# Local attention: weights split and stacked before the turn back, one spread matmul a shift, output read from PSUM, all query products on VectorE

## What is computed

```python
q = pointwise(Wq, bq, x); k = pointwise(Wk, bk, cond); v = pointwise(Wv, bv, cond)
k = pad(k, left 8, right 7); v = pad(v, left 8, right 7)
idx = arange(T)[:, None] + arange(16)[None, :]
k_win = k[:, :, idx].reshape(B, H, hd, T, W)
v_win = v[:, :, idx].reshape(B, H, hd, T, W)
dots = einsum('bhdt,bhdtw->bhtw', qh, k_win) * scale
attn = softmax(dots, axis=-1)
out = einsum('bhtw,bhdtw->bhdt', attn, v_win)
return pointwise(Wo, bo, out)
```

## Time and profile before

| | |
|---|---|
| median of 3 runs | 1247.41 us (1245.87 to 1249.03) |
| span of the profiled execution | 1249.7 us |
| VectorE busy | 958.3 us (77%) |
| TensorE matmuls | 1111.4 us (89%) |
| ScalarE | 290.6 us (23%) |
| GpSimd | 453.1 us (36%) |
| mean granted TensorE clock | 0.958 |

### The profile page before, as it was taken

One profiled execution on the slowest core, in us unless ns is written; L12 is line 12 of the kernel. 1 busy time (PEld: TensorE's weight loads), 2 busy tenths in 40 slices (PEclk: granted clock), 3 DMA queues, 4 the chain that ended last, 5 costly groups with the idle time before them and its releaser, 6 DMA issues. The chain is left out here.

```text
span 1249.7 us, 14398 instructions
## 1 busy us (share of the span) xinstructions
PE 1111.4 (89%) x5022; PEld 803.6 (64%) x5022; DVE 958.3 (77%) x1510; ACT 290.6 (23%) x442; POOL 453.1 (36%) x303
## 2 busy tenths in 40 slices
PE   5888888867778899998999989999999869999998
PEld 1433333334556777876778767877777646777687
DVE  5999999959977878877878778887887756666423
ACT  2222222113211222222222222232222221111122
POOL 5455555535515433432434233342442011112121
PEclk8899999888889999999999999999999969999999
DMA  8000000000301111101111011100100001212001
GB/s 266 1 1 3 1 2 1 9 9 11 105 28 34 52 34 35 52 7 47 34 34 37 15 52 35 34 32 20 61 7 1 1 17 53 65 54 56 14 1 68
DMA packets 45071, 43.26 MB, mean 35 GB/s; under 512 B 6574, under 2 KB 33974, under 8 KB 45004
## 3 DMA queue, kind: packets, MB, share of 16 engines
q1 hardware_dynamic: 44284, 41.70, 10.8%
q10 hardware_dynamic: 720, 0.63, 0.1%
HBM read 40.22 MB, written 2.10 MB: 34 GB/s over the span
## 5 line engine op out<-in xcount | busy, mean ns | idle before, releaser
L1171 POOL TENSOR_TENSOR shared<-shared 128x512 f32<-128x512 f32 x80 | 103.0, 1287 | 181.5 <-DVE shared L1298 181.5
L1176 POOL TENSOR_TENSOR s<-s,c_mx 128x256 f32<-128x256 f32 x64 | 39.3, 615 | 217.7 <-DVE c_mx L1315 217.7
L699 PE MATMUL ps<-woh,oh 128*128 128x512 f32 x256 | 104.8, 409 | 7.8 <-DVE ol L1345 7.6
L369 POOL TENSOR_TENSOR r<-r 128x1024 f32<-128x1024 f32 x32 | 77.3, 2417 | 88.8 <-DVE r L508 88.7
L700 PE MATMUL ps<-xl,wqh 128*128 128x512 f32 x256 | 102.1, 399 | 5.7 <-issue 5.7
L699 PE MATMUL ps<-xh,wqh 128*128 128x512 f32 x256 | 106.1, 414 | 0.4 <-DVE shared L1298 0.4
L701 PE MATMUL ps<-xh,wql 128*128 128x512 f32 x256 | 101.8, 398 | 0.0
L700 PE MATMUL ps<-wol,oh 128*128 128x512 f32 x256 | 101.2, 395 | 0.0
L701 PE MATMUL ps<-woh,ol 128*128 128x512 f32 x256 | 101.2, 395 | 0.0
L1329 DVE TENSOR_TENSOR bd<-s,c_rs 64x256 f32<-64x256 f32 x128 | 88.9, 694 | 4.2
L1456 PE MATMUL ps<-shared 128*128 128x128 f32 x512 | 68.9, 277 | 26.0 <-POOL shared L1171 25.9
(11 more groups left out here) (190 smaller groups left out, 2639.3 us busy)
## 6 DMA issues: line engine op xcount, KB each, us to landing
stage<-in_wq SPq DMA_DIRECT2D x16, 512.0 KB, 3.8
stage<-in_wo SPq DMA_DIRECT2D x16, 512.0 KB, 3.4
qraw<-in_gate_qweight SPq DMA_DIRECT2D x40, 64.0 KB, 2.3
qraw<-in_up_qweight SPq DMA_DIRECT2D x40, 64.0 KB, 2.3
qraw<-in_down_qweight SPq DMA_DIRECT2D x10, 256.0 KB, 3.4
x<-in_x SPq DMA_DIRECT2D x8, 256.0 KB, 7.5
ctxt<-in_ctx SPq DMA_DIRECT2D x8, 256.0 KB, 7.6
stage<-in_wk SPq DMA_DIRECT2D x8, 256.0 KB, 2.7
```

Of the source, the lines that this page charges most:

```text
L369: pool.tensor_tensor(r2[:, w:w + 2, :], r[:, w:w + 2, :], r[:, WIN // 2 + w:WIN // 2 + w + 2, :], ALU.add).then_inc(rsum_ready, 1)
L699: pe.matmul(dst, lh, rh, start=(first and c == 0), stop=False)
L1171: pool.tensor_tensor(dst, ra[:, r % 2, :], rb[:, r % 2, :], ALU.add).then_inc(rope_ready, 1)
```

## The change

1. The weights are split before they are turned back. ScalarE writes their rounded part (`high_half`) and GpSimd the rest (`low_half`), in halves of 8 shifts, into `stack`, where the rounded and the remaining part of four shifts fill 128 columns. TensorE turns 16 blocks of 128x128 in place of 8 (`turn_back`), and ScalarE copies each half out (`turned_half`). Both parts now lie on the partitions of one operand, so that a single matmul a shift spreads and adds them (`spread_window`).
2. All four q products are VectorE's.
3. ScalarE adds the output's bias to x ahead of time (`biased`), and VectorE adds the output from PSUM in one operation (`add_output`), now behind part 0 of the products and ahead of the sum of the exponentials.
4. The scores leave PSUM in two halves through one bank, q has a bank of its own, and keys and values are projected ahead of the queries.
5. TensorE's list: output pairs 0 and 1 of tile i stand in the ring behind shifts n = 10 and 14, pairs 2 and 3 at the start of the next round; the queries stand in the ring behind n = 4.
6. ScalarE's list in a round: exponential, keys and values, the two high parts, the first turned half, the first scores, the second turned half, the second scores, queries, biased x.
7. GpSimd's list: `scales_pool` comes first in a round, then the two low parts, then `scale_of_rows` and the four additions.

```diff
-        ath = sb("ath", [P, 2, D], F32R)
-        atl = sb("atl", [P, 2, D], F32R)
+        stack = sb("stack", [P, D // P, WBLOCKS, 2, GW * BH], F32R)
+        turned = sb("turned", [P, WBLOCKS, D], F32R)
...
-        o = sb("o", [P, D])
...
+        S, QB, M = ps[:, 0, :], ps[:, 1, :], ps[:, 7, :]
...
-        ORDER = [w + d for w in range(0, WIN // 2, 2) for d in (0, 1, WIN // 2, WIN // 2 + 1)]
-        RINGS = 2 + WIN
+        HALFW = WIN // 2
+        ORDER = [h + w + d for h in (0, HALFW) for w in range(0, GW, 2) for d in (0, 1, GW, GW + 1)]
...
+            def low_half(i, h):
+                pool.wait_ge(hi_ready, 2 * i + h + 1)
+                blocks = slice(2 * h, 2 * h + 2)
+                pool.tensor_tensor(stack[:, :, blocks, 1, :], half_windows(h), stack[:, :, blocks, 0, :].bitcast(F32),
+                                   ALU.subtract).then_inc(lo_ready, 1)
...
             for s in range(NT + 1):
-                if s < NT:
-                    pool.wait_ge(qkv_ready, 3 * s + 2)
-                    if s >= 1:
-                        pool.wait_ge(prod_used, 4 * s)
-                    products(pool, s, PARTS - 1).then_inc(last_prod_ready, 1)
-                if s + 2 < NT:
-                    scale_of_rows(s + 2)
+                i = s - 1
                 m, k = (s - 2) // 2, (s - 2) % 2
                 if 0 <= m < 3:
                     scales_pool(pool, g, m, k)
                 if s >= 1:
-                    i = s - 1
-                    for w in range(0, WIN // 2, 2):
-                        pool.wait_ge(r_ready, WIN * i + 2 * w + 4)
-                        if i >= 1 and w == 0:
+                    low_half(i, 0)
+                    low_half(i, 1)
+                if s + 2 < NT:
+                    scale_of_rows(s + 2)
+                if s >= 1:
+                    for m in range(WIN // 4):
+                        w = ORDER[4 * m]
+                        pool.wait_ge(r_ready, WIN * i + 4 * m + 4)
+                        if i >= 1 and m == 0:
                             pool.wait_ge(out_done, i)
...
+            def biased(i):
+                act.wait_ge(xn_ready, i + 1)
+                act.wait_ge(gate_ready, 2)
+                act.activation(x[:, i, :], x[:, i, :], ACT.Identity, bias=gbo[:, 0:1]).then_inc(xb_ready, 1)
...
+            def high_half(i, h):
                 if i >= 1:
-                    act.wait_ge(x_ready, i)
-                act.activation(o[:, :], M, ACT.Identity, bias=gbo[:, 0:1], scale=gate[:, 0:1]).then_inc(o_ready, 1)
-            project(0)
+                    act.wait_ge(back_done, 2 * (i - 1) + h + 1)
+                act.activation(stack[:, :, 2 * h:2 * h + 2, 0, :], half_windows(h), ACT.Copy).then_inc(hi_ready, 1)
+            def turned_half(i, h):
+                act.wait_ge(back_done, 2 * i + h + 1)
+                if i >= 1:
+                    act.wait_ge(spread_done, WIN * (i - 1) + HALFW * (h + 1))
+                act.activation(turned[:, 2 * h:2 * h + 2, :], T2, ACT.Copy).then_inc(turned_ready, 1)
+            def scores_out(i, grp):
+                act.wait_ge(prod_used, PARTS * i + 2 * (grp + 1))
+                if i >= 1 and grp == 0:
+                    act.wait_ge(fwd_done, i)
+                act.activation(sc[:, grp, :], S, ACT.Copy).then_inc(sc_ready, 1)
...
+            def add_output(i):
+                dve.wait_ge(out_done, i + 1)
+                dve.wait_ge(xb_ready, i + 1)
+                dve.scalar_tensor_tensor(x[:, i, :], M, gate[:, 0:1], x[:, i, :], ALU.mult, ALU.add).then_inc(x_ready, 1)
+                dve.wait_ge(x_ready, i + 1)
+                row_sums(dve, g, st, i)
...
-                    dve.wait_ge(qkv_ready, 3 * (s + 1))
                     part_of_products(s, 0)
-                    part_of_products(s, 1)
-                if s + 2 < NT:
-                    statistics(s + 2)
+                if s >= 2:
+                    add_output(s - 2)
...
-                    part_of_products(s, 2)
+                    for part in range(1, PARTS):
+                        part_of_products(s, part)
+                if s + 2 < NT:
+                    statistics(s + 2)
                 if 1 <= s <= NT:
-                    dve.wait_ge(ath_ready, s)
-                    dve.tensor_tensor(atl[:, :, :], T2, ath[:, :, :].bitcast(F32), ALU.subtract).then_inc(atl_ready, 1)
-                if s >= 2:
-                    i = s - 2
-                    dve.wait_ge(o_ready, i + 1)
-                    dve.tensor_tensor(x[:, i, :], x[:, i, :], o[:, :], ALU.add).then_inc(x_ready, 1)
-                    dve.wait_ge(x_ready, i + 1)
-                    row_sums(dve, g, st, i)
...
-            def output(i, pairs=range(WIN // 4)):
-                if i + 2 < NT:
-                    pe.wait_ge(qkv_ready, 3 * (i + 2) + 1)
+            def output(i, pairs):
                 for pair in pairs:
+                    if pair == 0 and i >= 1:
+                        pe.wait_ge(x_ready, i)
...
+            def turn_back(i, h):
+                pe.wait_ge(lo_ready, 2 * i + h + 1)
+                if h == 1:
+                    pe.wait_ge(turned_ready, 2 * i + 1)
+                for j in range(2):
+                    for b in range(D // P):
+                        last = pe.transpose(T2[:, j, b * P:(b + 1) * P],
+                                            stack[:, b, 2 * h + j, :, :].rearrange("p e m -> p (e m)").bitcast(F32), ident[:, :])
+                last.then_inc(back_done, 1)
+            def spread_window(i, n):
+                w = ORDER[n]
+                if n < 3:
+                    pe.wait_ge(kv_ready, 2 * min(i + 3, NT))
+                    pe.wait_ge(turned_ready, 2 * i + 1)
+                    if i >= 1:
+                        pe.wait_ge(r_ready, WIN * i)
+                else:
+                    pe.wait_ge(r_ready, WIN * i + n - 2)
+                if n == HALFW:
+                    pe.wait_ge(turned_ready, 2 * i + 2)
+                pe.matmul(RING[(2 + n) % 3], spread[:, w % GW, :], turned[:, w // GW, :], start=True, stop=True)\
+                  .then_inc(spread_done, 1)
...
+                    for n in range(3, WIN):
+                        spread_window(i, n)
+                        if n == 4 and s + 1 < NT:
+                            queries(s + 1)
+                        if n == HALFW and s < NT:
                             scores_turned(s)
-                        if s == NT and n in (10, 14):
-                            output(NT - 1, (n // 4 - 2,))
-                else:
-                    scores_turned(s)
+                        if n == 10:
+                            output(i, (0,))
+                        if n == 14:
+                            output(i, (1,))
...
+    for part in range(2):
+        for w in range(GW):
+            spread[(part * GW + w) * BH + ch // LHD, w, ch] = 1
```

More of the change, by code:

```diff
@@ L239, in windowed_attention @@
         sel = sb("sel", [P, 2, 32])
[L240 to L241 removed]
+        spread_f = sb("spread_f", [P, GW, P])
+        spread = sb("spread", [P, GW, P], F32R)
         xn = sb("xn", [P, 2, D])
@@ L517, in _, with keys_values @@
             pe.wait_ge(w4_landed, 16)
-            def project(i):
-                pe.wait_ge(xn_ready, i + 1)
-                if i >= 3:
-                    pe.wait_ge(o_ready, i - 2)
-                pe.matmul(M, w4[:, 0, :], xn[:, i % 2, :], start=True, stop=True).then_inc(qkv_done, 1)
+            def keys_values(i):
                 pe.wait_ge(ctx_landed[i], 16)
@@ L527, in project, with queries @@
                 for j in (1, 2):
-                    pe.matmul(RING[j - 1], w4[:, j, :], ctxt[:, i, :], start=True, stop=True).then_inc(qkv_done, 1)
-            def reduce_heads(i, part):
-                if part < PARTS - 1:
-                    pe.wait_ge(prod_ready, (PARTS - 1) * i + part + 1)
-                else:
-                    pe.wait_ge(last_prod_ready, i + 1)
-                if i >= 1 and part == 0:
-                    pe.wait_ge(sc_ready, i)
+                    pe.matmul(RING[j - 1], w4[:, j, :], ctxt[:, i, :], start=True, stop=True).then_inc(kv_done, 1)
+            def queries(i):
+                pe.wait_ge(xn_ready, i + 1)
+                if i >= 1:
+                    pe.wait_ge(q_ready, i)
+                pe.matmul(QB, w4[:, 0, :], xn[:, i % 2, :], start=True, stop=True).then_inc(q_done, 1)
+            def reduce_heads(i, part):
+                pe.wait_ge(prod_ready, PARTS * i + part + 1)
+                if part == 0 and i >= 1:
+                    pe.wait_ge(sc_ready, 2 * i)
+                elif part == 2:
+                    pe.wait_ge(sc_ready, 2 * i + 1)
                 for u in (2 * part, 2 * part + 1):
-                    dst = S[u // 4][32 * (u % 4):32 * (u % 4) + 32, :]
+                    dst = S[32 * (u % 4):32 * (u % 4) + 32, :]
                     pe.matmul(dst, sel[:, 0, :], prod[:, 2 * u, :], start=True, stop=False)
@@ L576, in _ @@
-                if s >= 1:
```

(25 more changed lines are left out.)

138 lines of the change are left out of this document (68 added, 70 removed).

## The result

The changed kernel takes 1258.86 us (median of 4 runs, 1257.04 to 1259.33) against 1247.75 on the same chip: ratio 1.0083, 95% interval [1.0059, 1.0107]. The profiled execution spans 1257.4 us. The forecast was 1263, in a range of 1250 to 1273.

A forecast was written before the change was run, and what follows sets the result against it. VectorE's own list, plus what GpSimd holds back, was taken to bound the first stage. Four steady rounds +12, other rounds +3.4, +1.7 and +0.2, start -1.7: +15.6 on the 1247.41 median gives 1263 us, range 1250 to 1273.

The forecast's parts named there:

- Step 1: Steady round: GpSimd's product moves to VectorE, products and statistics take 7.84 against 9.32 us, -1.5.
- step 4: Steady round: GpSimd's scales subtraction holds VectorE's first product 2.67 us; before, it held the division 0.85; net +1.8.
- Step 2: Steady round: low part leaves VectorE, x + o becomes one operation from PSUM, 2.74 us replaced by 0.75 and 0.65, -1.3.
- Step 3: Steady round: two GpSimd low-part subtractions, released during three back-to-back products, both come out of VectorE's time, +2.6.
- The rival that they cost nothing: Low parts get no turn between VectorE's products or run beside them: 18 us go, 1245 us; chance 0.11.
- lost the race: GpSimd's scales subtraction, leading by 0.13 us, comes behind VectorE's first product: 11.5 us less, 1251.5 us; chance 0.15.
- Step 5: The ring of 16 products: output pairs 0 and 1 inside it open two gaps of 0.8 us; ring 11.4 against 10.04, +1.4.
- Step 6: New chain from division to spread: hidden in steady rounds, product 3 reduced about 1.8 us behind it; 0.5 each in s = 6, 7.
- s = 1: Round s = 1: a steady round without the scales subtraction's 2.67 and 1.4 of x and its sums, 30.6 us, +3.4.
- the last round: Round s = 8: later addition and longer chain +2.4, shorter ring gaps -1.4, ScalarE's final pass (0.78 us) goes: +0.2.
- The start: Up to the first mx: fourth product no longer queues GpSimd ahead of VectorE, q projected last: -1.7, from 0 to -3.5.
- The clock rival: TensorE idles about 5 us for the low part, its clock falls, spread 3 comes late: +8, 1271 us; chance 0.17.

The follow-up runs named there:

- experiment 10: Kernel before with the fourth product on VectorE behind the third and GpSimd's scales subtraction behind VectorE's product 0: 1231.4 us, 0.9872.
- experiment 6: Changed kernel with the two low parts on VectorE, behind product 1, in place of GpSimd: 1252.43 us, 1.0031.
- experiment 8: Changed kernel with GpSimd's scales subtraction in the ring, low parts on VectorE, outputs at the next round's start, addition to x behind low parts: 1232.77 us, 0.9875.
- experiment 5: Changed kernel with GpSimd's scales subtraction moved behind the low parts and the ring's first product: 1250.51 us, 1.0011.
- experiment 11: Like experiment 10, but with GpSimd's scales subtraction straight behind the last addition of a round: 1242.61 us, 0.996.
- experiment 7: Changed kernel with all output pairs at the start of the next round, none in the ring except for the last tile: 1249.38 us, 1.0011.
- experiment 3: Changed kernel with 92 extra long-fulfilled wait instructions in TensorE's list ahead of the first reduction: 1274.63 us, 1.0209.
- experiment 4: Kernel before with 164 extra long-fulfilled wait instructions in TensorE's list ahead of the first reduction: 1244.74 us, 0.9971.
- experiment 9: Kernel of experiment 8 with GpSimd's scales subtraction behind VectorE's product 0, beside the row sum, not at the ring's start: 1219.78 us, 0.9774.
- 2: before, again: Kernel before with 128 empty instructions heading TensorE's list, which never reached the chip, so a second measurement: 1248.21 us, 1.0002.
- 1: after, again: Changed kernel with 128 empty instructions heading TensorE's list, which never reached the chip, so a second measurement: 1261.62 us, 1.0108.

## Why the prediction was right, step by step

The sign, the mechanism and most of the stage's steady part were right. Two sizes were wrong, and that they were of opposite sign is luck: the stage was 4.8 us worse than the sum, and the later stages, taken as untouched, gave 9 to 13 back. Had they stayed as they were, the stage's 20.4 us on top of the median of 1247.41 would have made 1268: still slower and in the range, but 5 us off on the other side.

- **Step 1**, the fourth product, -1.5: experiment 10 measured -2.6 a round for it together with an undisturbed division (0.85 in step 4). -2.35 was forecast for the two: right.
- **Step 2**, -1.3: 2.74 us in the earlier trace rows against 1.39 after, start to start (136.78 to 138.17), where 1.40 was forecast. Right, though not tested alone.
- **Step 3**, the low parts, +2.6: 8.83 less 6.75 is 2.1. The mechanism is right, the size 0.5 too high; why a little of each subtraction costs nothing was not looked into. Experiments 6 and 8 showed that the same work costs VectorE no more when it does it itself. The rival that they cost nothing is refuted.
- **Step 4**, L755, +1.8 with 2.67 for product 0: 4.79 less 2.28 is 2.5, confirmed by experiments 5 and 11. It never lost the race.
- **Step 5**, +1.4: 0.89 and 0.75 for two gaps; experiment 7 removed them by the outputs' place alone.
- **Step 6** was the weak one. The first spreads were indeed hidden in the steady rounds, but spread 3 was not "just ahead of when it is wanted": the reduction of product 3 ends 2.7 us behind it in the round above (150.6 to 153.36), not 1.8, and VectorE waits 0.27 to 0.94 us a round in the steady part, 1.66 and 1.45 in s = 6 and 7 where 0.5 was set. In s = 1, with no additions to x and no row sums as cover, VectorE waited 2.02 us at n = 0 and 1.69 at n = 3: that round grew by 5.6, not 3.4. And the last round grew by 2.5, not 0.2: where VectorE has no products to do, it waits for the whole chain, 6.10 us, and for an output that now ends in this round, 2.11.
- **The start**, -1.7: 29.07 to 27.53, -1.5.

Sum of the stage: 10.96 for four rounds (forecast 12), 5.59 (3.4), 2.90 (1.7), 2.47 (0.2), -1.54 (-1.7): 20.4.

**The clock rival** was there in every round, for less than it charged. TensorE in the round above, its timeline, then two rows of s = 2, and below them the stretches ahead of and over the turn back, as in the earlier trace rows:

```profile
145.25 1.97 PE L611 MATMUL ps<-ident,stack 128*128 128x128 f32 x8 [4.50 <-POOL stack L350]
147.14 1.73 PE L579 MATMUL ps<-prod,sel 128*32 128x512 f32 x4
148.70 1.03 PE L580 MATMUL ps<-prod,sel 128*32 128x512 f32 x4
...
150.46 1.03 PE L611 MATMUL ps<-ident,stack 128*128 128x128 f32 x8
...
77.77 1.93 PE L579 MATMUL ps<-prod,sel 128*32 128x512 f32 x4
79.48 1.43 PE L580 MATMUL ps<-prod,sel 128*32 128x512 f32 x4
...
142.00:145.20 3.20, 0.00 (x0) 0.00 (x0) 3.20 (x2) 1.05 (x2) 2.59 (x2) 0.99 0.00 0
145.20:147.20 2.00, 1.95 (x10) 1.62 (x12) 2.00 (x1) 0.00 (x0) 2.00 (x1) 0.50 0.00 0
```

After 4.5 us without work the turn back ran at a granted clock of 0.50, the lower level (1.2 GHz), and took 1.97 us where the next took 1.03. The Trainium skill, "TensorE: Matmul & The Clock Gate", section "HAM oscillation — how this bites in real kernels", says that behind such a gap TensorE's next work starts slow, and the trace agrees. But the clock came back within the round (0.93 over the steady part). The longer it stays low, the larger is the gap at n = 3: 0.37 us where the two reductions behind the turn back take 1.73 and 1.03, 0.94 in s = 2 where they take 1.93 and 1.43. The gaps at n = 3 make 6.9 us over rounds 1 to 7, where the sum had 1.0 and the rival 8 more. No run isolates the clock's share of them: the first turn back alone lost 0.94 us to it in the round above, but experiments 5 to 7 changed its cover and its neighbours too.

**What the sum had no term for** is instruction fetch: it took all behind 277 us as unchanged, with no reason given, and the 5.7 us at "issue" stood on the page of before. Experiments 3 and 4 show the cause. The table puts the stage's end and the span of each profiled execution side by side; what lies between them is work that none of the edits touches.

| kernel | packets of instructions | stage's end | span | between |
|---|---|---|---|---|
| before | 47 | 276.9 | 1249.7 | 972.8 |
| 2: before, again | 47 | 276.9 | 1246.2 | 969.3 |
| after | 28 | 297.3 | 1257.4 | 960.1 |
| 1: after, again | 28 | 297.0 | 1257.2 | 960.2 |
| 3: after, filled | 47 | 302.1 | 1272.8 | 970.7 |
| 4: before, filled | 29 | 286.6 | 1245.1 | 958.5 |
| 5: L815 in the ring | 28 | 291.0 | 1249.1 | 958.1 |
| 6: low parts on VectorE | 28 | 294.0 | 1252.0 | 958.0 |
| 7: outputs ahead of the ring | 28 | 286.8 | 1244.7 | 957.9 |
| 8: 5, 6 and 7 together | 28 | 271.7 | 1230.9 | 959.2 |
| 9: fastest | 28 | 256.8 | 1215.9 | 959.1 |
| 10: product alone | 47 | 260.3 | 1228.2 | 967.9 |
| 11: product, L755 first | 47 | 272.5 | 1241.1 | 968.6 |

The two levels are 958 to 960 and 968 to 973, and the packets go with them in all thirteen profiles. So the fourth product on VectorE, with L755 out of its way, is worth some 16 us (experiment 10), and the place at which TensorE's shorter list puts the later loop 8 to 13. The first is what the change meant to do, the second is luck. What turned the two into a loss are L815's place, the low part on GpSimd and the outputs inside the ring. Of the 11.6 us by which experiment 9 beats experiment 10, the stage itself gives 3.5 (256.8 against 260.3) and the rest lies behind it: the turned and stacked weights are worth that little once all is well placed. A kernel 10 with its loops moved was not run. Which loop's turn meets which boundary was counted, not traced. Levels within a group differ by up to 5 us, 3.5 of it between two profiles of the kernel before, and the rest stays open.

## What to carry to other kernels

Before moving work to GpSimd, look what VectorE does meanwhile. A VectorE operation with two inputs in SBUF and a GpSimd operation were not done side by side here, so such work costs the bound engine its time even on the other engine. Put it beside operations that read PSUM, or beside a reduction as in experiment 9, and last of all check what it pushes back on its own queue. A shorter chain of matmuls is worth nothing where a new link lies between two engines and nothing covers it: look at the first and the last rounds, where the cover is missing. And when code ahead of a loop changes length, compare the instruction queue's packets and the waits for issue before crediting or blaming the edit.

## What the runs showed of the hardware

- The place of a loop in TensorE's list moves its time: 47 or 28 packets of instructions, two waits for issue of together 5.5 to 6.6 us at one line and two of together 0.8 to 1.5 at another. In the kernel before they fall on two turns of the loop and go with a lower clock (0.88 granted from 580 to 590 us), and each turn came 5.4 and 6.6 us later for it.
- Filling is not free. 164 fulfilled wait instructions ahead of TensorE's first reduction moved the first mx by 7.5 us in the kernel before, 92 in the changed kernel by 1.4.
- The normalising reads x from SBUF with per-row scalars, and it was held 3.0 us by GpSimd's additions, past one boundary between two of them (148.3), to the end of the last. So a waiting operation does not always get the next turn. The row sum, which reads one SBUF operand too, was not held by GpSimd's subtraction (1.88 us in experiment 9, 1.86 in the changed kernel, where GpSimd does nothing meanwhile); what sets the two apart no run shows.
- A VectorE product with GpSimd work queued behind it holds GpSimd likewise: a subtraction of 2.80 us took 4.79.
